# Two transformer blocks on one core: each stage prepares the first tile of the layer norm of the stage behind it

## What is computed

```
def layer_norm(x, g, b):
    mu = jnp.mean(x, axis=-1, keepdims=True)
    var = jnp.mean(jnp.square(x - mu), axis=-1, keepdims=True)
    return (x - mu) * jax.lax.rsqrt(var + EPS) * g + b
...
h = layer_norm(hidden_states, norm1_g, norm1_b)
hidden_states = attention(h, h, attn1_wq, attn1_wk, attn1_wv, attn1_wo, attn1_bo) + hidden_states
h = layer_norm(hidden_states, norm2_g, norm2_b)
hidden_states = attention(h, encoder_hidden_states, attn2_wq, attn2_wk, attn2_wv, attn2_wo, attn2_bo) + hidden_states
h = layer_norm(hidden_states, norm3_g, norm3_b)
proj = h @ ff_w1 + ff_b1
a, gate = jnp.split(proj, 2, axis=-1)
hidden_states = a * jax.nn.gelu(gate, approximate=False) @ ff_w2 + ff_b2 + hidden_states
```

## Time and profile before

| what | value |
|---|---|
| runs | 4155.46, 4156.39, 4149.88 us, median 4155.46 |
| profiled execution | 4145.4 us, of which the span of the trace is 4143.5 |
| mean granted clock of PE in it | 0.959 of full speed |
| busy, share of the span | PE 93%, PEld 58%, DVE 65%, ACT 57%, POOL 45% |

### The profile page before, as it was taken

The page is one execution under the profiler, slowest core; times in us unless marked ns, Lnnn a source line. Parts: engine busy times, 40 slices in busy tenths (PEclk is TensorE's granted clock), DMA queues, the critical chain, the costliest instruction groups (busy, mean ns, idle before and its releaser), DMA issues. The chain is left out here.

```text
span 4143.5 us, 63013 instructions
## 1 busy us (share of the span) xinstructions
PE 3840.2 (93%) x23695; PEld 2393.1 (58%) x23695; DVE 2706.8 (65%) x4469; ACT 2378.2 (57%) x3310; POOL 1859.0 (45%) x1202
## 2 busy tenths in 40 slices
PE   3799999995989997997999999999999969999899
PEld 2533443433557886885555555555555547777787
DVE  6599999953537654435676666666666537665665
ACT  1477777781543333445777777777777744443332
POOL 1278891001203102004878878878887843222200
PEclk9789999996889998999999999999999979999999
DMA  4745333405622006884222222222222110000100
GB/s 159 187 57 76 63 53 50 46 2 95 110 39 59 18 12 210 306 309 146 77 82 92 77 82 91 79 82 74 90 77 82 47 40 9 3 10 1 43 16 16
DMA packets 314173, 328.15 MB, mean 79 GB/s; under 512 B 129592, under 2 KB 232952, under 8 KB 309520
## 3 DMA queue, kind: packets, MB, share of 16 engines
q1 hardware_dynamic: 311216, 315.17, 28.6%
q0 software_dynamic: 2656, 8.97, 0.8%
HBM read 195.47 MB, written 127.55 MB: 78 GB/s over the span
## 5 line engine op out<-in xcount | busy, mean ns | idle before, releaser
L1814 POOL TENSOR_TENSOR f_sums<-f_sums,f_probs 128x1024 f32<-128x1024 f32 x384 | 916.7, 2387 | 113.8 <-ACT f_probs L1952 75.6
L1831 DVE TENSOR_REDUCE f_mx<-f_s 128x1 f32<-128x512 f32 x992 | 635.0, 682 | 338.5 <-PE f_s L1977 330.7
L1952 ACT ACTIVATE f_probs<-f_st 128x1024 f32<-128x1024 f32 x512 | 520.3, 1016 | 321.7 <-PE f_st L2021 321.3
L1503 ACT ACTIVATE f_probs<-f_st 128x512 f32<-128x512 f32 x1024 | 535.9, 601 | 168.1 <-PE f_st L1561 167.9
L1372 DVE TENSOR_REDUCE f_mx<-f_s 128x1 f32<-128x512 f32 x960 | 600.0, 683 | 30.3 <-PE f_s L1523 7.9
L1920 ACT ACTIVATE f_st<-f_shift 128x1024 f32<-128x1024 f32 x512 | 526.6, 1029 | 23.4 <-DMA f_shift<-shift 7.2
L2037 PE MATMUL f_acc<-f_probs,f_v 128*64 128x512 f32 x2048 | 494.0, 603 | 0.0
L1977 PE MATMUL f_s<-f_k,f_q 64*128 64x512 f32 x2976 | 479.3, 412 | 4.7 <-DVE f_mx L1831 4.7
L1977 PEld LDWEIGHTS f_s<-f_k,f_q 64*128 64x128 f32 x2976 | 268.2, 184 | 245.2 <-DVE f_mx L1831 127.8
L2021 PE MATMUL f_st<-f_q,f_k 64*128 64x512 f32 x3072 | 399.2, 390 | 5.2 <-ACT f_st L1920 5.2
L1561 PE MATMUL f_st<-f_q,f_k 50*128 50x512 f32 x1024 | 332.9, 473 | 6.9 <-ACT f_probs L1503 6.8
(11 more groups left out here) (355 smaller groups left out, 7847.8 us busy)
## 6 DMA issues: line engine op xcount, KB each, us to landing
q<-f_stage SPq DMA_DIRECT2D x80, 512.0 KB, 2.8
k<-f_stage SPq DMA_DIRECT2D x80, 512.0 KB, 2.8
f_q<-q SPq DMA_DIRECT2D x32, 1024.0 KB, 5.0
f_k<-k SPq DMA_DIRECT2D x32, 1024.0 KB, 7.4
f_shift<-shift SPq DMA_DIRECT2D x32, 1024.0 KB, 4.7
v<-f_v_stage SPq DMA_DIRECT2D x64, 256.0 KB, 3.1
f_v<-v SPq DMA_DIRECT2D x32, 512.0 KB, 4.0
f_q<-q SPq DMA_DIRECT2D x96, 128.0 KB, 4.3
```

The lines of the kernel that those rows point to most:

```text
L1503: a_.activation(probs[:, n % NP, e % 2, :], stb[k % 3][:, :], ACT.Exp, scale=L.scale).then_inc(p_ready, 1)
L1814: g_.tensor_tensor(out, out, probs[:, n % NP, :, :], ALU.add).then_inc(sum_done, 1)
L1831: v.tensor_reduce(mx[:, i % 2, c:c + 1], bank[u % 3][:, :], AX_X, ALU.max).then_inc(s_free, 1)
L1952: a_.activation(probs[:, s % NP, :, :], stb[s % 2][:, :, :], ACT.Exp, scale=L.scale).then_inc(p_ready, 1)
```

## The change

Two things are done. First, gain and shift of all six norms are loaded in quantise: twelve DMAs of 256 single elements each, issued by SP behind the load of x, into one buffer that lives through the program; SP waits for them at the end of quantise. The loads of g and b at the head of each norm's stage, and ACT's waits for them, are gone.

Second, there is one more set of norm buffers that lives through the program (`first`). The stage ahead of each norm's stage works out statistics, inverse root and normalised rows of tile 0 into it; the norm's stage begins with the transposes of tile 0, which read first["xhat"]. In place of the removed instructions the stage counts its semaphores up (take_first, skip_first). Each first_rstd writes its constants as well (one more memset row in six places). Where the three parts stand:

| stage that does it | DVE statistics | POOL first_rstd | DVE normalised rows |
|---|---|---|---|
| quantise | behind the reductions and a wait for x, ahead of `top` | start | at its very end |
| context_kv | first | first | behind the splitting of its inputs |
| cross_narrow | unit 42 of 64 | 44 | 46 |
| feed_forward L0 | tile 4, chunk 1 | behind tile 5's | tile 4, chunk 5 |
| attend_wide | last step, b == 1 | last step, behind sum n == 4 | last step, b == 4 |
| cross_block | 41 of 64 | 42 | 46 |

```diff
@@ quantise
                 sp.dma_start(x_sb[:, :, :], ins["x"].rearrange("b (k p) d -> p (b k) d", p=P)).then_inc(x_in, 16)
+                for k, (gain, shift) in enumerate(self.norms):
+                    for j, src in enumerate((gain, shift)):
+                        sp.dma_start(self.gains[:, k, j, :], ins[src].rearrange("(c p) -> p c", p=P), allow_slow_non_contiguous=True)\
+                            .then_inc(g_in, 16)
...
+                sp.wait_ge(g_in, 32 * len(self.norms))
...
+                self.first_rstd(pool, ahead_norm)
...
                     step.done(v.tensor_reduce(ext[0:rows, K + j:K + j + 1], part(w, j), AX_X, ALU.min, negate=True))
+                dve.wait_ge(x_in, 16)
+                self.norm_stats(dve, ahead_norm, x_sb, 0)
                 dve.wait_ge(ext_t, 1)
                 step.done(v.tensor_reduce(top[:, :], pt[:, :], AX_X, ALU.max))
...
                 assert step.n == STAGES, step.n
+                self.norm_xhat(dve, ahead_norm, x_sb, 0)
@@ helpers
+    def first_buffers(self, sem):
+        n = dict(self.first)
+        n["chain"], n["pool_chain"], n["turned"] = sem("first_chain"), sem("first_pool"), None
+        return n
+    def first_rstd(self, pool, n):
+        self.norm_constants(pool, n)
+        self.norm_rstd(pool, n, 0)
+    def take_first(self, dve, n):
+        dve.sem_inc(n["chain"], self.STATS_STEPS)
+    def skip_first(self, pool, n):
+        pool.sem_inc(n["pool_chain"], self.RSTD_STEPS)
@@ norm_project (feed_forward alike)
-                self.norm_load(sp, n, g, b)
...
-                self.norm_rstd(pool, n, 0)
+                self.skip_first(pool, n)
...
-                self.norm_stats(dve, n, x_sb, 0)
-                self.norm_xhat(dve, n, x_sb, 0)
+                self.take_first(dve, n)
...
                 high(0)
-                act.wait_ge(n["gb_in"], 32)
                 self.norm_scale(act, n, 0)
@@ attend_wide
+                            if n == 4 and i == STEPS - 1:
+                                self.first_rstd(pool, ahead_norm)
...
+                        if i == STEPS - 1 and b == 1:
+                            dve.wait_ge(s_free, at["y", L.ng - 1, 0, 1] + 1)
+                            self.norm_stats(dve, ahead_norm, x_sb, 0)
+                        if i == STEPS - 1 and b == PER_HALF:
+                            self.norm_xhat(dve, ahead_norm, x_sb, 0)
@@ cross_block
+                    if n == 41:
+                        dve.wait_ge(y_done, y_last)
+                        self.norm_stats(dve, ahead_norm, x_sb, 0)
+                    if n == 46:
+                        self.norm_xhat(dve, ahead_norm, x_sb, 0)
```

More of the change, by code:

```diff
@@ L431, in late_quantise, with context_kv @@
             pool.wait_ge(s["out"][k], 16 * ((len(pieces) + 1 - k) // 2))
-    def context_kv(self, L, wk, wv):
+    def context_kv(self, L, x_sb, wk, wv):
         nc = self.nc
@@ L539, in norm_buffers @@
                   [sb(f"h_lo{k}", [P, DC, self.TT], F32R) for k in range(2)]]
-        n["g"], n["b"] = sb("g", [P, DC]), sb("b", [P, DC])
-        for s in ("gb_in", "chain", "mv_done", "rstd_done", "pool_chain", "xhat_done", "turned", "ht_done",
+        for s in ("chain", "mv_done", "rstd_done", "pool_chain", "xhat_done", "turned", "ht_done",
                   "cut_done", "hi_done", "lo_done", "used"):
@@ L618, in norm_turn @@
             for j in range(self.TB):
-                ins = self.nc.tensor.transpose(n["tp"][:, c, j * P:(j + 1) * P], n["xhat"][:, j, c * P:(c + 1) * P],
+                rows = self.first["xhat"] if t == 0 else n["xhat"]
+                ins = self.nc.tensor.transpose(n["tp"][:, c, j * P:(j + 1) * P], rows[:, j, c * P:(c + 1) * P],
                                                ident[:, :])
@@ L2361, in cross_narrow @@
             bank = [ps(f"r{k}", [P, 512]) for k in range(RING)]
-            gb_in, w_in, wo_in, b_in, set_done, biased = (sem(s) for s in ("gb_in", "w_in", "wo_in", "b_in", "set", "biased"))
+            w_in, wo_in, b_in, set_done, biased = (sem(s) for s in ("w_in", "wo_in", "b_in", "set", "biased"))
             kv_in, vraw_in = [sem(f"kv_in{k}") for k in range(B)], [sem(f"v_raw_in{k}") for k in range(B)]
@@ L2623, in norm_turn @@
                         for j in range(TB):
-                            ins = t_.transpose(bank[u % RING][:, j * P:(j + 1) * P], xhat[:, j, c * P:(c + 1) * P], ident[:, :])
+                            rows = self.first["xhat"] if t == 0 else xhat
+                            ins = t_.transpose(bank[u % RING][:, j * P:(j + 1) * P], rows[:, j, c * P:(c + 1) * P], ident[:, :])
                         ins.then_inc(r_ready, 1)
@@ L2817, in cross_block @@
                 h = [[sb(f"h_{part}{k}", [P, DC, TT], F32R) for k in two] for part in ("hi", "lo")]
-            gam, bet = sb("g", [P, DC]), sb("b", [P, DC])
+            gam, bet = g, b
+            ahead_norm = self.first_buffers(sem)
+            y_last = max(nth(*key) for key in at if key[0] == "y" and key[1] == 0)
             wraw, oraw = sb("wraw", [P, DC * L.dim]), sb("oraw", [P, OCH * D])
@@ L2958, in _ @@
                         zero(n)
+                    if n == 42:
+                        self.first_rstd(pool, ahead_norm)
                     if n == 3 and not narrow:
@@ L3125, in turn @@
                         for j in range(TB):
-                            ins = t_.transpose(bank[u % 4][:, j * P:(j + 1) * P], xhat[:, j, c * P:(c + 1) * P], ident[:, :])
+                            rows = self.first["xhat"] if t == 0 else xhat
+                            ins = t_.transpose(bank[u % 4][:, j * P:(j + 1) * P], rows[:, j, c * P:(c + 1) * P], ident[:, :])
                         ins.then_inc(r_ready, 1)
@@ L3238, in feed_forward @@
             sb, ps, sem = self.open(st)
-            n = self.norm_buffers(sb, ps, sem)
+            n = self.norm_buffers(sb, ps, sem, (g, b))
+            ahead_norm = None if store else self.first_buffers(sem)
             raw = [sb(f"raw{k}", [P, PIECE]) for k in range(STAGES)]
@@ L3328, in _ @@
                     self.norm_rstd(pool, n, t)
+                    if ahead_norm and t == 5:
+                        self.first_rstd(pool, ahead_norm)
                     if ahead and t == 2:
@@ L3386, in _ @@
                         self.norm_xhat(dve, n, x_sb, t + 1)
+                    if ahead_norm and (t, j) == (4, 1):
+                        dve.wait_ge(y_done, 2)
+                        self.norm_stats(dve, ahead_norm, x_sb, 0)
+                    if ahead_norm and (t, j) == (4, 5):
+                        self.norm_xhat(dve, ahead_norm, x_sb, 0)
                     if j == 6 and t + 1 < TILES:
@@ L3527, in build @@
             self.late_sems = [st.enter_context(nc.semaphore(f"late_{x}{k}")) for x in ("in", "out") for k in range(2)]
+            self.norms = [("L0_xattn_ln1_g", "L0_xattn_ln1_b"), ("L0_xattn_ln2_g", "L0_xattn_ln2_b"), ("L0_xattn_ln3_g", "L0_xattn_ln3_b"),
+                          ("L1_xattn_norm1_g", "L1_xattn_norm1_b"), ("L1_xattn_norm2_g", "L1_xattn_norm2_b"),
+                          ("L1_xattn_norm3_g", "L1_xattn_norm3_b")]
+            self.gains = st.enter_context(nc.sbuf_tensor("norm_gains", [P, len(self.norms), 2, DC], F32))
+            shapes = dict(stats=[P, self.TB, 6], const=[P, 3, self.TB], xhat=[P, self.TB, D])
+            for k in ("sum", "diff", "m2", "mean", "var", "ve", "rstd", "tmp"):
+                shapes[k] = [P, self.TB]
+            self.first = {k: st.enter_context(nc.sbuf_tensor("first_" + k, shape, F32)) for k, shape in shapes.items()}
             self.quantise(x_sb, ident)
+            gains = [(self.gains[:, k, 0, :], self.gains[:, k, 1, :]) for k in range(len(self.norms))]
             def p(name):
```

65 lines of the change are left out of this document (32 added, 33 removed).

## The result

The changed kernel took 4133.06 us (median of 4, from 4122.20 to 4135.77) against 4155.82 for the one before (median of 4); the ratio is 0.9937, with a 95% interval of 0.9915 to 0.9959. Measured a second time, on the chip of the first experiments, it was 0.9914 (0.9883 to 0.9945). Faster was right, but 10.3 us were forecast and 22.8 and then 34 were measured. The two profiled spans differ by 15.0 us, 4143.5 and 4128.5.

A forecast was written before the change was run, and what follows sets the result against it. PE, busy 93% of the span, bounds the kernel, so gains lie in its waits. Heads win 20.9 us, costs take 10.6: net 10.3 less, median from 4155.46 to 4145.2; range 4133 to 4158.

The forecast's parts named there:

- heads: Starts of the six norm stages, up to the first scaling or transposes: shorter by 20.9 us in all.
- inserted pieces: Norm work of tile 0 placed in the stage ahead: costs 10.6 us in all, including the clock's fall.
- a start made shorter moves everything behind it: At each norm stage's head: time won there carries through, as long as the same engine chain goes on.
- Quantise +3.5: In quantise: DVE waits for x and does statistics ahead of `top`, so the stage ends 3.5 us later.
- a forecast of 5.35: Last step of attend_wide: PE's wait for the sums grows from 2.45 to 5.35 us behind the inserted inverse root.
- The term for the clock: In attend_wide behind the longer wait: PE at half the clock for 5 us, costing 2.5 us.
- cross_block +1.6: At unit 41, inserted statistics delay the next maximum and subtraction by 2.2 us; with 0.6 slack, PE loses 1.6.
- A: Rival: the clock stays up in attend_wide; net 12.8 us less, 4142.7; chance 0.25.
- B: Rival: what is late next swallows part of the heads' gain; net 4.3 us, 4151.2, within 0.2%; chance 0.3.
- C: Rival: in quantise the twelve single-element loads delay x by up to 25 us; net -14.9, 4170.3; chance 0.06.
- D: Rival: heads wait for something all stages need anyway, as in cross_block; chance no more than a part of B.
- The 3 us that I allowed for runs: Allowance in the forecast range for how far medians of few runs move: some 3 us.

The follow-up runs named there:

- e7: Kernel before with 192 unused bytes behind g and b in every stage with a norm, so weights begin at a multiple of 256; ratio 0.9976.
- e4: Changed kernel with 64 unused bytes where g and b stood, so weights lie 64 bytes beyond a multiple of 256 again; ratio 0.9972.
- e2: Kernel before with only the gain and shift loads moved to quantise; the norm of tile 0 stays in its own stage; ratio 0.9970.
- e5: Changed kernel without its piece in attend_wide; cross_block's norm of tile 0 is back at that stage's head; 4121.26 us, ratio 0.9917.
- e8: As e5, with cross_block's statistics, inverse root and rows at units 43, 44, 50 and quantise's statistics behind the extremes' way over PE; 4117.62 us, ratio 0.9902.
- c1: The kernel before, run again with no edit; ratio 1.0014.
- e1: Kernel before with the change's lasting buffers (about 4.5 KB a partition) only allocated and not used; ratio 0.9990.
- e3: Kernel before with 64 unused bytes behind g and b in every stage with a norm; ratio 0.9998.

## Why the prediction was wrong

**The step that failed** is that the sum held only heads and inserted pieces: "a start made shorter moves everything behind it". It had no term for what the edit does to instructions that it leaves alone. Removing g and b moved the weights to a multiple of 256 bytes, and e7 gives the size of that by itself, 7.6 us in norm_project L1 and about 10 in all. e4, without it, is 12 us faster than before, near the 10.3 of the sum. As both have intervals of several us, that shows the size and not the exact figure. The removal of the two buffers was in the diff; I read it as the removal of two DMAs.

**The heads.** norm_project L1 5.6 (5.55 forecast), feed_forward L1 2.7 (2.9), feed_forward L0 2.6 (2.75) and cross_narrow 2.9 (3.2) by the first row that matters. norm_project L0 gave 6.4 instead of 5.55 and cross_block 1.5 instead of 0.95: in this pair the weights came not only 0.93 earlier, they were also used sooner after their own issue, 2.65 instead of 3.35 us in norm_project L0. I had kept the old 3.35, and it was the longest of the five profiles that have g and b ahead of the weights (2.82 to 3.35; the nine others have 2.65 to 2.85). So this part is in the main the spread of a landing, not a gain of the change. In cross_block the first use of the weights is also not all: by tile 2's transposes, at 59.5 instead of 63.4, its head gave 3.9 us, nearly all of it from the loads (3.7 in e2). Why so much was not traced.

**The costs.** Quantise +3.5 was measured as +3.5. attend_wide: a wait of 5.41 for a forecast of 5.35; from this wait's end to the stage's end it took 34.90 us instead of 34.35, so 3.5 us in the profiled pair instead of 5.4. The term for the clock, 2.5 us, was 0.55 in this pair. Over all profiles it was nearer: the way to the end took 34.6 to 37.1 us in the six with the piece (mean 36.0) and 33.6 to 34.4 in the eight without (mean 34.0). In e5 and e8 the stage is 3 us or more shorter than in any profile with the piece. cross_block +1.6: the wait right to 0.1, the clock's fall behind it missed, 3 to 5 us in four of seven profiles. The Trainium skill, "TensorE: Matmul & The Clock Gate", section "Why this matters for your kernels", warns of idle gaps between bursts of matmuls, and I had put that against the long wait only. The traces agree that the clock falls behind gaps, but a gap's length doesn't decide it: behind the same 1.52 us in cross_block the clock fell to 0.50 in four profiles and stayed at 1.00 in three, and behind 2.45 us in attend_wide it was 1.00 in the kernel before, and 0.66 over 5 us behind an equal wait, at 3293.7, in the changed one.

**The rivals.** A, the clock staying up in attend_wide, did not happen in any of the six profiles with the piece (0.50 to 0.73 over the 5 us behind the wait). B, that what is late next swallows the gains, did not either in the heads. C fell: x was used at 30.33, and 30.2 was forecast for its landing, so the twelve loads behind it did not hold it up. Its sum is also off by 0.2: with 25 us it gives -14.7, and the -14.9 written goes with 25.2. D held for cross_block alone, as said; its piece in attend_wide buys nothing that the profile of e5 shows.

**The range** began at 4133, and the measured median is 4133.06. That it lies inside is luck, since the sum lacked about 10 us; the second measure, 4124.76, lies outside. Of the 34 us measured there some 10 are the addresses and 10.3 were forecast. The other 14 were not traced to a cause. They are within the 18 us by which attend_narrow alone differs between two executions of one kernel. The 3 us that I allowed for runs came from three executions.

## What to carry to other kernels

When an edit adds or removes a buffer, list the addresses of the buffers behind it, and compare the duration of an instruction that was not changed; if it moved, measure the edit once more with the old place restored by unused bytes. An address that helps one stage may do nothing for the next, as norm_project and feed_forward show here. A piece of work that is moved into "idle" slots of an engine should go into the slot that is emptiest, not the next one, since here a stall of PE of 1.5 us cost three to four times that in four profiles of seven, through the clock. Where the head of a stage waits for a large load anyway, as in cross_block, preparing its norm ahead bought nothing and cost what it displaced.

## What the runs showed of the hardware

- The matmuls of norm_project L1 (fp32r, 128x512) took 389 ns in the median where the weights began at a multiple of 256 bytes, and 394 where they began 64 or 128 beyond one, with the tile period 2.5% apart (33.53 and 34.4 us). It held for both uses, the weights as the held operand (f_pc) and as the moved one (f_pv: 389 against 394 to 396), and it was the same in all nine profiles of the one kind and all five of the other. The Trainium skill, "SBUF — State Buffer", section "Operand start alignment", asks only for a multiple of the element size and says that its rule is about what is legal and not about speed; the traces show that in this stage the speed depends on the start as well.
- In cross_block the same shift is worth 0.3 us of 53.5 a tile (53.2 in the kernels with a multiple of 256), and in feed_forward L1 nothing (306.7 in e7, 306.6 to 307.1 in c1, e1 and e3).
- One kernel on one core has two lengths of attend_narrow, 783 to 789 and 795 to 804 us, and in c1 the clock was 0.68 over the 60 us in which it was 1.00 in the first profile.
- Two loads of 256 single elements ahead of the 1 MB of weights of cross_block cost their 0.95 us of issue; from their own issue to their first use these weights took 5.15 to 5.68 us behind such loads (five profiles) and 4.92 to 5.25 without them (nine), ranges that overlap.
- In cross_block the same wait of PE of 1.52 us was followed by a clock of about 0.5 in four profiles and of 1.00 in three.
